# A perceiver megakernel on one core: small exact products of the first experts' stage gathered on TensorE, with new orders on VectorE and ScalarE

## What is computed

```python
# attention with phases (hidden_states is the normed x)
qp = hidden_states @ Wtq.T + btq                      # two phases a token
dist_sq = sum((qp_i - qp_j) ** 2)
threshold = mean(dist_sq) + 1.25 * std(dist_sq, ddof=1)
valid = (dist_sq <= threshold) & causal
masked = where(valid * forward_bias(qp) == 0, -inf, q @ k.T / sqrt(d))
output = (softmax(masked) @ v) @ Wo.T + bo
r_embed = qp / max(norm(qp), 1e-12)
x = x + hidden_states + output + 0.1 * (r_embed @ Wfq.T + bfq)
# experts (xf is the normed x)
topk_s, topk_i = top_k(xf @ gate_w + gate_b, 2)       # comb: scores of the two chosen, else 0
h = relu(xf @ w1[e] + b1[e]); eo = h @ w2[e] + b2[e]  # 8 experts
x = x + sum_e comb[:, e] * eo
```

## Time and profile before

| | |
|---|---|
| median of 3 runs | 648.8 us (647.76 to 650.24) |
| profiled execution | 648.06 us, span of its instructions 646.3 us |
| TensorE (PE) busy | 590.4 us, 91% of the span |
| weight loads (PEld) | 457.9 us, 71% |
| VectorE (DVE) | 467.7 us, 72% |
| ScalarE (ACT) | 371.5 us, 57% |
| GpSimd (POOL) | 240.7 us, 37% |

### The profile page before, as it was taken

How to read it: one execution, slowest core, us unless ns; L and a number is a source line. 1 busy time by engine, 2 the same in 40 slices (tenths; PEclk the granted TensorE clock), 3 DMA queues, 4 the chain that set the end, 5 groups by cost and what they waited for, 6 DMA issues and landing times. The chain is left out here.

```text
span 646.3 us, 11821 instructions
## 1 busy us (share of the span) xinstructions
PE 590.4 (91%) x4476; PEld 457.9 (71%) x4476; DVE 467.7 (72%) x810; ACT 371.5 (57%) x701; POOL 240.7 (37%) x194
## 2 busy tenths in 40 slices
PE   8999999999998778878788999999999899999997
PEld 6655555564466667767677889987777667889897
DVE  3753333347777999999999538789977878886554
ACT  3311111137989999999999534344656465556342
POOL 2000000000099999999899230036641022231000
PEclk9999999999999999999999999999999999999999
DMA  9999999995813222233320000000100022210100
GB/s 327 417 419 422 419 421 423 417 351 181 246 34 100 99 99 99 98 100 124 103 98 2 2 1 13 6 2 18 37 3 3 1 65 83 65 50 1 33 2 32
DMA packets 31103, 87.53 MB, mean 135 GB/s; under 512 B 8140, under 2 KB 20904, under 8 KB 27080
## 3 DMA queue, kind: packets, MB, share of 16 engines
q1 hardware_dynamic: 30360, 86.20, 36.2%
q10 hardware_dynamic: 688, 0.59, 0.3%
HBM read 84.55 MB, written 1.11 MB: 133 GB/s over the span
## 5 line engine op out<-in xcount | busy, mean ns | idle before, releaser
L853 POOL TENSOR_TENSOR dbu<-du,bs 128x1024 f32<-128x1024 f32 x64 | 149.8, 2366 | 7.1 <-DVE w_in L1101 4.7
L982 ACT ACTIVATE weighed<-T,CT 128x256 f32<-128x256 f32 x222 | 95.3, 596 | 1.2 <-PE T L1180 0.9
L1101 DVE TENSOR_TENSOR_SCAN w_in<-hS,dbu 128x1024 f32<-128x1024 f32 x42 | 94.6, 2273 | 0.4 <-ACT hS L971 0.4
L971 ACT ACTIVATE hS<-delta,negA 128x504 f32<-128x504 f32 x128 | 91.0, 817 | 5.3 <-DVE xn L1101 2.5
L1194 PE MATMUL Y<-ident,weighed 128*128 128x128 f32 x512 | 66.8, 273 | 0.1
L1180 PE MATMUL T<-ident,w_in 128*128 128x128 f32 x336 | 46.0, 279 | 19.9 <-ACT weighed L982 13.8
L1194 PEld LDWEIGHTS Y<-ident,weighed 128*128 128x128 f32 x512 | 57.8, 141 | 0.9 <-DVE sres L1125 0.3
L1180 PEld LDWEIGHTS T<-ident,w_in 128*128 128x128 f32 x336 | 36.1, 140 | 30.8 <-DVE w_in L1101 27.4
L1101 DVE TENSOR_TENSOR_SCAN xn<-hS,dbu 128x1024 f32<-128x1024 f32 x22 | 50.1, 2276 | 2.3 <-ACT hS L971 2.3
L430 POOL COPY w_xp<-w_xp 128x64 f32<-128x64 f32 x3 | 0.6, 236 | 136.9 <-DMA w_out<-in_w_out 136.9
L305 PE MATMUL S<-cT,qkT 128*64 128x512 f32 (+1 forms) x256 | 44.8, 502 | 6.0 <-DMA cT<-in_ctxT 6.0
(11 more groups left out here) (464 smaller groups left out, 1364.0 us busy)
## 6 DMA issues: line engine op xcount, KB each, us to landing
cN<-in_ctx SPq DMA_DIRECT2D x8, 3072.0 KB, 25.8
cT<-in_ctxT SPq DMA_DIRECT2D x7, 3202.0 KB, 26.0
bs<-b_rows SPq DMA_DIRECT2D x32, 512.0 KB, 3.7
raw_w<-in_w SPq DMA_DIRECT2D x16, 256.0 KB, 2.8
cT<-in_ctxT SPq DMA_DIRECT2D x2, 1089.0 KB, 10.1
cR<-in_ctx SPq DMA_DIRECT2D x8, 256.0 KB, 26.1
w<-in_w SPq DMA_DIRECT2D x7, 256.0 KB, 8.1
vs<-vx SPq DMA_DIRECT2D x8, 136.0 KB, 2.5
```

What stands on the lines that cost most here:

```text
L853: e.tensor_tensor(dbu[s % NB][:, :, :], half(m.du, s // DS), row, ALU.mult).then_inc(s_bu, 1)
L971: i = e.activation(by_batch(A[s % 2][:, j * HALF:(j + 1) * HALF]), by_batch(m.delta[:, c, h * HALF:(h + 1) * HALF]), ACT.Exp, scale=m.negA ...
L982: i = e.activation(weighed[s % 2][:, q * Q:(q + 1) * Q], T[:, q * Q:(q + 1) * Q], ACT.Copy, scale=c_of(s, q))
L1101: e.tensor_tensor_scan(S[s % NS], A[s % 2][:, :], dbu[s % NB][:, :, :].rearrange("p c n -> p (c n)"), 0.0, ALU.mult, ALU.add).then_inc(s_h, 1)
```

## The change

TensorE: the second attention half's values are no longer split and no expert step stands between gates, values, sum, turnings, sum of squares and scores; the first shares follow in one run. In `hidden` all blocks' products with the large part of x come ahead of the wait for `x_lo`. The bank of the first pair of first shares changes from 2 to 6, and `output(0)`'s first pair no longer waits for their addition. VectorE: `bias_parts` moves behind `rest_of_hidden(0)`, the phases' norms get a function of their own ahead of `choose(0)`, `masks` is cut into `variances`, `cones` and the rest. ScalarE: order of matrices 5 to 7 and of the moves.

```diff
-        SH = ((2, 3), (6, 7))
+        SH = ((6, 3), (6, 7))
@@ pe_steps, ac_steps, mask_steps: the same names in the new order
@@ hidden
                         e.matmul(HB[m][:, :], k.w_lo[x][:, 0, c, cols], k.x_hi[:, c, tok], start=False, stop=False)
-                    if x == 0:
-                        e.wait_ge(s_xl, 2 * (h + 1))
+                if x == 0:
+                    e.wait_ge(s_xl, 2 * (h + 1))
+                for m in blocks:
+                    cols = slice(m * P, (m + 1) * P)
                     for c in range(KD):
                         i = e.matmul(HB[m][:, :], k.w_hi[x][:, 0, c, cols], k.x_lo[:, c, tok], start=False, stop=c == 1)
@@ output
-                    e.wait_ge(s_a, 2 * n + g + 1)
+                    if n or g:
+                        e.wait_ge(s_a, 2 * n + g + 1)
@@ TensorE's list
             hidden(0)
+            hidden(1)
             scores_of_experts(0, 0)
-            hidden(1, [0])
             scores_of_experts(0, 1)
-            hidden(1, [1])
             values(1, 0)
             batch_sum()
+            values(1, 1)
             turn_shares(0)
-            values(1, 1, [0])
+            turn_phases()
+            batch_squares()
+            scores(1)
             first_shares(0, 0)
-            values(1, 1, [1])
             first_shares(0, 1)
-            batch_squares()
             output(0)
-            scores(1)
             hidden(2)
-            turn_phases()
             output(1)
             hidden(3)
             turn(1)
             project_phase(0)
+            project_phase(1)
             output(2)
-            project_phase(1)
             hidden(4)
...
             hidden(7)
+            output(6, [0])
             scores_of_experts(1, 0)
-            output(6, [0])
             scores_of_experts(1, 1)
@@ ScalarE's list
             rectify(0)
             large(4)
             rectify(1)
+            large(5)
             move_values(1, 0)
+            large(6)
+            move_values(1, 1)
             shares_across(0)
-            move_values(1, 1)
-            large(5)
-            large(6)
+            move_phases()
+            spread()
             large(7)
-            spread()
-            move_phases()
             rectify(2)
@@ VectorE: spreads() loses its first part to directions() (nrmx, nri, re); masks() loses var to variances()
@@ and ady0, ady, ok to cones(); the list
             small_part(0)
-            bias_parts()
             rest_of_normed(0)
             small_part(1)
             distances()
             rest_of_hidden(0)
+            bias_parts()
+            directions()
             choose(0)
+            spreads()
             rest_of_hidden(1)
-            spreads()
+            variances()
             add_shares(0)
+            cones()
+            add_output(0)
             masks()
-            add_output(0)
+            shift(1)
             rest_of_hidden(2)
-            shift(1)
+            add_output(1)
             add_normed()
-            add_output(1)
-            rest_of_hidden(3)
             denominators(1)
             add_phases(0)
+            add_phases(1)
+            rest_of_hidden(3)
             add_output(2)
-            add_phases(1)
             rest_of_hidden(4)
```

More of the change, by code:

```diff
@@ L2480, in phase_and_experts @@
         pe_steps = [("scores", 0), ("v", 0, 0), ("pT", 0), ("v", 0, 1), ("pv", 0, 0), ("pv", 0, 1), ("qk", 0), ("qp",),
-                    ("qk", 1), ("row",), ("v", 1, 0), ("sum",), ("v", 1, 1), ("sumsq",), ("scores", 1), ("reT",),
+                    ("qk", 1), ("row",), ("v", 1, 0), ("sum",), ("v", 1, 1), ("reT",), ("sumsq",), ("scores", 1),
                     ("pT", 1), ("pf", 0), ("pf", 1), ("pv", 1, 0), ("pv", 1, 1)]
         ac_steps = [("exp0", 0), ("exp", 0), ("v", 0, 0), ("pT", 0), ("v", 0, 1), ("qk", 0), ("qk", 1), ("nrm",),
-                    ("v", 1, 0), ("v", 1, 1), ("std",), ("reT",), ("exp0", 1), ("exp", 1), ("pT", 1)]
+                    ("v", 1, 0), ("v", 1, 1), ("reT",), ("std",), ("exp0", 1), ("exp", 1), ("pT", 1)]
         phase_steps = [("qp",), ("qsq",), ("nrm2",), ("diag",)]
         row_steps = [("dd",), ("dq",), ("dist",), ("rowsum",)]
-        mask_steps = [(n,) for n in ("nrmx", "nri", "re", "mean", "dev", "devsq", "rowsq", "ady0", "ady", "var", "ok", "okc",
+        mask_steps = [(n,) for n in ("nrmx", "nri", "re", "mean", "dev", "devsq", "rowsq", "var", "ady0", "ady", "ok", "okc",
                                      "thr", "in", "ok2", "add")]
@@ L2937, in distances, with directions @@
                 done(e.reduce_sum(rowsum[:, hs], dist[:, hs, :], AX.X), "rowsum")
-            def spreads():
+            def directions():
                 hs = half(1)
@@ L2945, in spreads @@
                                             nrm[:, 1, hs].unsqueeze(2).to_broadcast([P, HT, 2]), ALU.mult, ALU.mult), "re")
+            def spreads():
+                hs = half(1)
                 pe("sum")
@@ L2950, in spreads, with variances, cones @@
                 done(e.reduce_sum(rowsq[:, hs], dev[:, hs, :], AX.X), "rowsq")
-            def masks():
+            def variances():
                 hs = half(1)
+                pe("sumsq")
+                e.wait_ge(s_ve, ve_at["rowsq",])
+                done(e.tensor_scalar(var[:, hs], BK[SUMS][:, 128:128 + HT], 1.0 / (n_pairs - 1.0), None, ALU.mult), "var")
+            def cones():
                 o, a = ok[1][:, :, :], ady[:, :, :]
@@ L2956, in masks @@
                 chain(e.scalar_tensor_tensor(a, dd[:, 1], 4096.0, a, ALU.mult, ALU.max), "ady")
-                pe("sumsq")
-                e.wait_ge(s_ve, ve_at["rowsq",])
-                done(e.tensor_scalar(var[:, hs], BK[SUMS][:, 128:128 + HT], 1.0 / (n_pairs - 1.0), None, ALU.mult), "var")
                 chain(e.scalar_tensor_tensor(o, dd[:, 0], -1.0, a, ALU.mult, ALU.is_le), "ok")
+            def masks():
+                hs = half(1)
+                o = ok[1][:, :, :]
                 chain(e.tensor_tensor(o, o, k.causal[:, :].unsqueeze(1).to_broadcast([P, HT, L]), ALU.mult), "okc")
```

## The result

| | before | changed |
|---|---|---|
| median of 9 runs | 648.80 us (647.76 to 650.24) | 651.78 us (650.39 to 652.82) |
| profiled execution, span | 648.06, 646.3 us | 650.39, 648.7 us |

The changed kernel is slower: ratio 1.0043, 95% interval 1.0034 to 1.0052, or 2.8 us of 648.8. Its median lies above the forecast (648.7) and above its range (646.8 to 650.4), though inside the 0.5% that the chances called no change.

A forecast was written before the change was run, and what follows sets the result against it. TensorE's list was taken to bound the last stage. Terms: -0.73 + 0.20 + 1.13 - 0.73 = -0.13 us, taking the profiled 648.06 to 647.9; predicted median 648.7, range 646.8 to 650.4.

The forecast's parts named there:

- term 1: TensorE, joints between kinds of product: dear joints fall from 1.30 to 0.57 us, a gain of 0.73.
- term 2: TensorE, hidden(0) and hidden(1): the wait moves from x_lo to ScalarE's rectified values, a loss of 0.2 us.
- term 3: TensorE at the sum of squares: waits for row sums because GpSimd holds VectorE's dev or its square; loss 1.13 us.
- term 4: TensorE at the turning of the probabilities: the wait for the exponentials goes, a gain of 0.73 us.
- three signs of being wrong: New profile: dev and its square take 0.42 us each, share turning waits for VectorE, or hidden(1) starts without a wait.
- hidden(8) with its small parts last: TensorE's hidden(8): block 0 is rectified later, but under output(7)'s 2.87 us, so it costs nothing.
- edits at nothing: Remaining reorderings on TensorE, VectorE, ScalarE and the SP queue, costed at nothing; without cover each would cost below 1 us.
- The prediction's other count: TensorE joints with 24-row or 64-column products, counted by the Trainium skill alone: at 0.19 us each, gain 0.57.
- its cast alone may lose 0.2: VectorE's choose beside GpSimd's work on matrix 5: only its cast might be slowed, by 0.2 us.
- rival C: VectorE's choose is also held by GpSimd, so row sums come later: 649.9 us, slower than before; chance 0.15.
- rivals A to C: A: row-sum wait eats the gains, 0.55; B: GpSimd misses dev and its square, 647.5 us, 0.25; C: choose held, 0.15.
- dev might pass but hardly its square: VectorE beside GpSimd ahead of the row sums: by the skill's exclusive lock, dev might escape but its square hardly.

The follow-up runs named there:

- g: Run d with the new product order kept only in hidden(0) and hidden(8), where it waits for x_lo; 647.71 us, ratio 0.9978 to the kernel before.
- a: Changed kernel with the old order of products inside every hidden step (block 0 whole, then block 1); 648.20 us, ratio 0.9976 to the kernel before.
- d: Changed kernel with old product order in hidden and matrices 5 and 6 rounded later; 647.52 us, ratio 0.9965 to the kernel before.
- f: Run d with scores(1) put between the two pairs of first shares; 647.79 us, ratio 0.9978 to the kernel before.
- c: Changed kernel with ScalarE's matrices 5 and 6 rounded behind the moves of values, shares and phases; 650.74 us, ratio 1.0013 to the kernel before.
- e: Kernel before with only VectorE's bias parts moved behind x_lo; 649.06 us, ratio 0.9997 to the kernel before.
- b: Kernel before with only the new order of products inside every hidden step; 650.68 us, ratio 1.0016 to the kernel before.

## Why the prediction was wrong

The forecast was 0.1 us less than before; it came 2.8 us more. By the traces, 1.9 of that miss lie behind the turning of the probabilities, and 0.8 in front of it (0.66 lost where 0.13 were to be gained: term 1 gave 0.04 more than forecast, term 2 cost 0.23 more and term 3 0.60 more, term 4 came as forecast). Two of the prediction's own three signs of being wrong came: dev and its square took 0.42 and 0.43, and the turning of the shares waited for VectorE.

- **The step that failed: the split loop of `hidden`, priced only in "Term 2: the first hidden products" and as "hidden(8) with its small parts last" among the edits at nothing.** The prediction took the split loop to act where the wait is, in hidden(0) and hidden(8). Only the wait has the condition `x == 0`; the loop doesn't. So steps 1 to 7 and 9 to 15 were costed at nothing without being named, and behind the turning of the probabilities they hold 1.9 us. Hidden(8) itself was rightly put at nothing, as g shows. Taking the split back everywhere (a) gave 3.5 us by the spans; the prediction had a net loss of 0.20 there. The profile of before had the rows for it: block 0's relu starts as soon as its bank is done, and the wait for `w_lo` stood at the end of a path that starts with that relu.
- **Term 2 itself** was right in its mechanism: the wait for x_lo vanished and one for h_hi came, 0.99 us. From the spread rows' end to the end of hidden(1), the gates left out, it lost 0.43 us, not 0.20. The first product of hidden(1) was 0.06 later than forecast, and that of block 1 took 0.17 more, since it waited for its own h_hi (536.62 + 0.70 = 537.32, the product at 537.37). What I missed is that the order with the block first needs no such wait once x_lo comes early, as a and d show. It isn't free there either: hidden(0) and hidden(1), 24 products, take 6.1 us instead of 24 x 0.23 = 5.5, with short waits for x_lo and h_hi that the list of waits doesn't show.
- **Term 1** was right: from the end of values(1,0) to the end of output(1), 542.79 to 556.98 (14.19 us) before, run d needs 543.46 to 556.88, 13.42, so 0.77 gained where 0.73 was forecast. Gathering gates gave nothing, as read. The entry to 24-row products is 0.19, measured in f. The prediction's other count, six joints before and three after, 0.57, would have been further off.
- **Term 3** had the right conflict and the wrong victim. 1.13 us were forecast for dev or its square. In the changed kernel the casts of choose met GpSimd instead, and from the end of the second values' product (544.95) to that of the sum of squares (547.73) passed 2.77 us where d needs 1.04: 1.73 lost. In a, dev and GpSimd started within 0.01 us of the forecast (T + 1.22 and T + 1.23), dev passed and the square was held; the row sums came at T + 3.50 instead of T + 3.67, and by comparison with d that cost 0.97, where 1.13 were forecast. That the casts were caught in the changed kernel follows from the failed step: the prediction put GpSimd's work on matrix 5 at T - 1.6 to T - 0.3, and in a it ran from T - 1.62 to T - 0.35, but in the changed kernel it ran from T - 0.93 to T + 0.33, because ScalarE got through the relus of hidden(1) later: at T - 1.52, against T - 2.21 in a and T - 2.22 in g, where hidden(1) isn't split. The sentence "its cast alone may lose 0.2" is the mis-sized one: the first cast lost 0.67 and the second, which I had not looked at, 1.05. The loss on the first also put the second in matrix 6's way. It was a mild form of rival C, without the maxima and searches, which were not held (in a all four maxima and all four searches ran beside a subtraction, in 0.37 us and 0.16 each).
- **Term 4** was right: the four turnings took 0.44 and had no wait.
- **The chances**: rivals A to C all put the risk before 561 us. None looked at the path relu, rounding, subtraction, next expert.

The Trainium skill (SBUF — State Buffer, Who interferes with whom) says that a VectorE operation with two SBUF inputs contends with a GpSimd instruction that reads SBUF, that a cast can contend when its operands meet the conditions of a two-port mode, and that on this chip a reduction never does. The square at 1.38 us and the casts at 0.85 and 1.32 us agree with it, and so do c's 0.18 and 0.27 and two reductions in the changed kernel (at 560.87, 0.83 for both) beside a subtraction of 560.19 to 562.07. The prediction's sentence that dev might pass but hardly its square is what run a shows.

## What to carry to other kernels

When a loop is split for the sake of one wait, ask what it does in every iteration that has no wait: the time at which an accumulation's first block ends is an output of the loop like any other, and relus, roundings and rests hang on it. When a subtraction on GpSimd is moved, list every VectorE operation in its window by what it reads, casts included, and not only the ones on the path you are looking at; moving the rounding that triggers it behind the moves was worth 1.9 us in the changed kernel (c), and some 0.7 to 1.0 with the old order of products (d against a, by ratios whose intervals overlap and by spans). A wait removed early in a list is only worth what the next asker leaves of it: e gained 0.75 us and lost it at the next step.

## What the runs showed that was not expected

- A cast of 32 elements a partition, 0.18 us alone, took 0.85 us beside a GpSimd subtraction, and a pair of casts 1.32 instead of 0.27; index searches of the same size beside it kept their 0.16.
- A VectorE operation that starts 0.01 us ahead of GpSimd's takes its full 0.42, and the GpSimd operation is lengthened from 1.29 to 1.54; the next VectorE operation of the chain, 0.03 us later, is then held for the rest.
- The first product of hidden(1) started 0.14 to 0.15 us behind h_hi's end in the changed kernel and in a, b and d, against 0.05 for that of block 1 in the changed kernel, also released by h_hi, and 0.04 for one released by VectorE's x_lo in the kernel before. No run shows why.
